# A graph layer and a mixture of experts on one core: the result is built up in the output tensor itself

## What is computed

```
x = x + gnn(layernorm(x), edges, relations)
x = x + ffn(layernorm(x))

# ffn, for the rows xf [6250, 256] of one batch
_, idx = jax.lax.top_k(xf @ Wg + bg, 2)
mask = one_hot(idx, 8).sum(axis=-2)
h = gelu(einsum('td,edh->teh', xf, W1) + b1[None], approximate=False)
y = einsum('teh,ehd->ted', h, W2) + b2[None]
out = einsum('ted,te->td', y, mask)
```

## Time and profile before

| what | value |
|---|---|
| median of 3 runs | 1563.23 us (1562.03 to 1563.25) |
| the profiled execution's own time | 1562.57 us |
| its span, first to last instruction | 1560.7 us |
| time around the span | 1.87 us |
| expert part: first addition issued to last addition issued | 1219.7 to 1534.5 us |
| busy share of the span: PE, DVE, ACT, POOL | 83%, 65%, 47%, 64% |

### The profile page before, as it was taken

One profiled execution on the slowest core, in us unless ns is written; L12 is line 12 of the kernel. 1 busy time (PEld: TensorE's weight loads), 2 busy tenths in 40 slices (PEclk: granted clock), 3 DMA queues, 4 the chain that ended last, 5 costly groups with the idle time before them and its releaser, 6 DMA issues. The chain is left out here.

```text
span 1560.7 us, 36074 instructions
## 1 busy us (share of the span) xinstructions
PE 1292.3 (83%) x12887; PEld 1056.9 (68%) x12887; DVE 1013.0 (65%) x2768; ACT 732.4 (47%) x1489; POOL 993.0 (64%) x868
## 2 busy tenths in 40 slices
PE   1269998999999999998899998775572999999991
PEld 1145566777777777777777777665562899999990
DVE  7857765576677777777878886864344555555550
ACT  6424453555455555554334342322131767676660
POOL 2077764676667777777777777777732455555551
PEclk9659998999999999999999999887675999999996
DMA  9686632444444555454544543443933466555556
GB/s 292 177 208 188 182 89 84 140 135 127 132 121 134 141 138 148 132 146 119 142 129 133 140 134 109 116 125 115 328 82 96 70 96 96 94 95 91 96 79 185
DMA packets 132379, 209.99 MB, mean 135 GB/s; under 512 B 26552, under 2 KB 99837, under 8 KB 130919
## 3 DMA queue, kind: packets, MB, share of 16 engines
q0 software_dynamic: 60032, 112.63, 30.7%
q1 hardware_dynamic: 72167, 94.97, 20.9%
HBM read 158.70 MB, written 57.76 MB: 139 GB/s over the span
## 5 line engine op out<-in xcount | busy, mean ns | idle before, releaser
L716 POOL DMA_INDIRECT ring<-h_table,idx x648 | 680.4, 1050 | 296.0 <-issue 211.3
L1728 PE MATMUL P<-hs,amat 128*126 128x512 f16 (+4 forms) x1568 | 403.6, 391 | 0.0
L833 ACT ACTIVATE amat<-P 128x300 f16<-128x300 f32 (+4 forms) x440 | 175.9, 445 | 253.7 <-PE P L1715 252.2
L770 POOL DMA_INDIRECT out_rows<-yo,xrows x112 | 177.0, 1580 | 162.2 <-DVE yo L1592 110.0
L1728 PEld LDWEIGHTS P<-hs,amat 128*126 128x126 f16 (+4 forms) x1568 | 182.4, 130 | 92.9 <-issue 7.8
L1710 PE MATMUL P<-cone,lone 128*128 128x294 f16 (+4 forms) x920 | 182.0, 294 | 44.7 <-ACT amat L833 39.0
L725 POOL DMA_INDIRECT expert_rows<-xrow,slots x100 | 126.3, 1263 | 67.9 <-DVE slots L1335 38.1
L1583 DVE SCALAR_TENSOR_TENSOR gl<-gT,scales,gh 128x512 f16<-128x512 f32 x112 | 84.2, 752 | 127.7 <-ACT gh L960 127.7
L1192 DVE TENSOR_TENSOR cone<-src_t,twice 128x1176 f16<-128x1176 f16 (+4 forms) x230 | 164.4, 715 | 0.0
L1942 PE MATMUL P<-xh,w_all 128*128 128x256 f16 x896 | 157.8, 275 | 0.0
L1955 PE MATMUL P<-w_all,gh 128*128 x896 | 149.8, 273 | 0.7 <-DVE gl L1583 0.7
(11 more groups left out here) (244 smaller groups left out, 2751.4 us busy)
## 6 DMA issues: line engine op xcount, KB each, us to landing
raw<-in_L_ffn_W_dram SPq DMA_DIRECT2D x32, 512.0 KB
xrows<-expert_rows SPq DMA_DIRECT2D x56, 257.0 KB, 3.1
ring<-h_table,idx POOLq DMA_INDIRECT x648
w_parts<-parts SPq DMA_DIRECT2D x16, 512.0 KB
w_all<-w_parts SPq DMA_DIRECT2D x8, 1024.0 KB, 20.2
h_in<-h_table SPq DMA_DIRECT2D x25, 250.0 KB
x<-in_x_dram SPq DMA_DIRECT2D x25, 250.0 KB
out_rows<-x SPq DMA_DIRECT2D x25, 250.0 KB
```

The source lines that it names most:

```text
L716: nc.gpsimd.indirect_dma_start(out=ring[:, r, j, :], out_offset=None, in_=h_dram, in_offset=bass.IndirectOffsetOnAxis(ap=idx[:, slot, g * ...
L770: nc.gpsimd.indirect_dma_start(out=out_dram, out_offset=bass.IndirectOffsetOnAxis(ap=xrows[:, b % XR, j, D:D + 1].bitcast(I32), axis=0), i ...
L833: nc.scalar.activation(amat[:, b % 2, :, s * aw:(s + 1) * aw], bank[:, 0:HIS * aw].rearrange("p (h w) -> p h w", w=aw), ACT.Copy).then_inc ...
L1728: nc.tensor.matmul(both, amat[:, b % 2, hi, 0:used], hs[:, hi, :], start=(hi == 0), stop=False)
```

## The change

The kernel's own output takes the place of `out_rows` everywhere: SP stores the residual rows to `out`, and POOL adds the experts' rows to `out`. As `out` has no rows beyond 6250, each of the 112 indirect transfers gets a bound of 6249 (`bounds_check=N - 1`), held in a register, with `oob_is_err=False`: a row whose number lies above the bound is left out. The transfer that zeroed the extra rows, the extra rows themselves, and the copy at the end with its wait are gone. SP's last act is now the wait for the last additions, which stood ahead of the copy before. No other instruction of any engine changes or changes its place: the same waits stand between the same instructions.

```diff
-PADS = TB
...
-    out_dram = nc.dram_tensor("out_rows", [N + PADS, D], F32).ap()
...
-            sp.dma_start(out_dram[N:N + PADS, :].rearrange("(j p) d -> p j d", p=128), pads[:, :, 0:D]).then_inc(s_init, 16)
...
-                sp.dma_start(node_rows(out_dram, i), x1[:, :, :]).then_inc(x_stored, 16)
+                sp.dma_start(node_rows(out, i), x1[:, :, :]).then_inc(x_stored, 16)
...
-            sp.wait_ge(s_init, 16 * (NE + 2))
+            sp.wait_ge(s_init, 16 * (NE + 1))
...
             for n in range(2):
                 sp.wait_ge(y_added[n], 32 * ((BLOCKS + 1 - n) // 2))
-            flat_out = out.rearrange("n d -> (n d)").rearrange("(a m) -> a m", m=1000)
-            flat_rows = out_dram[0:N, :].rearrange("n d -> (n d)").rearrange("(a m) -> a m", m=1000)
-            sp.dma_start(flat_out, flat_rows).then_inc(out_written, 16)
-            sp.wait_ge(out_written, 16)
...
                 for j in range(2):
                     nc.gpsimd.indirect_dma_start(
-                        out=out_dram, out_offset=bass.IndirectOffsetOnAxis(ap=xrows[:, b % XR, j, D:D + 1].bitcast(I32), axis=0),
-                        in_=yo[:, b % 2, j, :], in_offset=None, compute_op=ALU.add).then_inc(y_added[b % 2], 16)
+                        out=out, out_offset=bass.IndirectOffsetOnAxis(ap=xrows[:, b % XR, j, D:D + 1].bitcast(I32), axis=0),
+                        in_=yo[:, b % 2, j, :], in_offset=None, compute_op=ALU.add,
+                        bounds_check=N - 1, oob_is_err=False).then_inc(y_added[b % 2], 16)
```

More of the change, by code:

```diff
@@ L500, in gnn_ffn_kernel @@
             tx_done xh_ready xl_ready w1_ready l1_done gelu_done g_high g_low l2_done y_out firsts_ready
-            out_written dve_chain late_chain
+            dve_chain late_chain
         """.split()
@@ L514, in gnn_ffn_kernel @@
          tx_done, xh_ready, xl_ready, w1_ready, l1_done, gelu_done, g_high, g_low, l2_done, y_out, firsts_ready,
-         out_written, dve_chain, late_chain) = [sem(n) for n in names]
+         dve_chain, late_chain) = [sem(n) for n in names]
         s_nat = [sem(f"s_nat{n}") for n in range(3)]
```

## The result

The changed kernel takes 1542.54 us in the median of 6 runs (1534.12 to 1553.89), the kernel before 1562.22 (1558.48 to 1563.25, 6 runs). The ratio is 0.9879, with a 95% interval of 0.985 to 0.9907: 19 us less, between 15 and 23. The prediction was 1540.5 us, within 1534.0 to 1544.5, so the time lies 2 us above it and inside the range. Over all runs of this study both kernels scatter by 15 us and more, so the steps are read from the profiles.

What follows compares the result with a forecast made beforehand. The prediction took PE to set the pace in the expert part and the copy alone to fill the end; -22.3 + 0.9 - 1.0 - 0.3 = -22.7 us from 1563.23 gave 1540.5 us, range 1534.0 to 1544.5.

Steps and rivals of the forecast that it cites:

- (a): End of the kernel: with the copy gone, SP's wait for the additions becomes the last thing, -22.3 us.
- (b): Bound test on POOL's additions: 0.15 us each, covered in steady blocks, +0.9 us for six in the tail (0 to +3.2).
- (c): Pad rows left out: two tail landings shorten by half the packet time, 2 x 0.5 = -1.0 us.
- the 16 to 18 of the forecast: Tail: expected us for the chain from block 53's second addition to the end, 16.75 before the change.
- the first rival: Tail: skipped additions are nearly free, chain 12 to 13 us, time 1531 to 1538; chance 0.20.
- My test by the number of packets: Software queue, expert part: 14,292 packets if left-out rows have none; 16,128 would mean skipping saves nothing on the DMA engines.
- The rival of nearly free skips: Tail: skipped additions lose most of their landings, perhaps part of POOL's time; 1531 to 1538 us, chance 0.20.
- (d): Ahead of the expert part: without zeroing the spare rows, first gathers may come forward, -0.3 us (0 to -1.1).
- My condition that a move of over 2 us would mean an overlooked cause: Expert part's start: first addition expected at 1218.6 to 1219.7; moving over 2 us means something upstream isn't unchanged.
- a dear bound: POOL's additions: the test costs more but within POOL's slack, 0.7 us at most; 1543 to 1560 us, chance 0.08.
- POOL as the bound and a slower kernel: Expert part: test above 0.70 us an addition makes POOL set the pace, gain gone at 0.9 us; chance 0.04.

## Why the prediction held, and where it didn't

**(a) The copy, -22.3 us.** The length of the copy was right, and the step that failed is "Nothing lies beside it, so here the share of the copy on the path is all of it", with "SP's wait for the additions [...] becomes the last thing". POOL's DRAIN had ended 4.6 us after the additions landed, under the copy; now it is the end, 5.8 us behind SP in the changed kernel. The term's net is 22.3 - 5.8 = 16.5 us. The experiments without the copy and with another last instruction on POOL show it. The rows for it could have been had: the instructions of the program's end, with their start and duration, are in the trace of the kernel before, but they count as no engine's busy time, and I read only what was busy. Additions to the output tensor land no later than those to the scratch tensor: from block 53's second addition to block 54's first are 4.73 us, and 4.83 in the kernel before with the same bound.

**(b) The bound, +0.9 us in the tail.** The comparison's price is nothing: an addition takes 1.56 us with and without. The more software work for each row that the prediction drew from the Trainium skill ("DMA: Bandwidth & Descriptors", section "SWDGE vs HWDGE vs iDMA") shows in no run; the section states a pair of descriptors for a DMA operation, and that each row is one was the prediction's reading, which the 128 + 16 packets of an addition fit. What the bound does cost is 0.5 us between DVE's result and a block's first addition, since its register's setting took over the wait. POOL's slack covers that in the steady blocks, as I had said of any such price; in the tail it counts once, for block 53, which waits for DVE. So +0.5.

**(c) Skipped rows, -1.0 us.** Measured 1.0 for each of the two landings, so -2.0 up to SP's release: about the whole of the packets' time, where I had taken half. The chain from block 53's second addition to that release is 14.8 us, below the 16 to 18 of the forecast and above the 12 to 13 of the first rival. But the end follows POOL's last addition and not its landing, so block 55's microsecond is one that SP waits longer for the DRAIN, and only block 54's shortens the time. My test by the number of packets was built on a wrong idea: the number stayed at 16,128 and the packets became short. The rival of nearly free skips is answered with it: POOL spends the full time on skipped rows, and the landing keeps 1.2 to 1.3 us behind POOL's 1.56. The Trainium skill ("DMA: Bandwidth & Descriptors", section "Anatomy of one DMA") puts most of a transfer's fixed 2 us down to the receipt of the write. No such share fell away: the landing became 1.0 us shorter, and the 1.1 us by which the packets' time fell account for that. What the 1.2 to 1.3 us that are left consist of, no run shows.

**(d) The zeroing, -0.3 us.** Not settled: the start of the expert part moved by 3.4 us between the two profiles, by up to 1.7 us between profiles of one kernel, and by 5.1 and 8.5 us within the kernels with and without the zeroing. My condition that a move of over 2 us would mean an overlooked cause was too strict for a single profile.

With the terms as measured, -16.5 + 0.5 - 2.0 = -18.0 us. Counted by what ends last it is the same: the copy's removal -17.5 (22.3, less the 4.6 and the 0.2 us that POOL's DRAIN and the end behind it take back), the displaced wait +0.5, one landing -1.0. The profiles differ by 18.0 us from DVE's first result on. This lies in the measured -15 to -23 and within a microsecond of the median ratio's -19. The forecast of -22.7 was 4 to 5 us too much. That the time fell within the range is luck: it did because the range reached 4 us upwards for quite another reason, a dear bound, and because the median of before over six runs lies 1.0 us below the one that the sum started from. From that start the terms as measured give 1563.23 - 18.0 = 1545.2 us, just outside the range. POOL as the bound and a slower kernel are refuted: POOL idles 2.25 us a block as before.

## What to carry to other kernels

When the last thing on the path is taken away, look at everything that it covered, and at each engine's last instructions too, which no busy time shows: the gain is the distance to the next thing that ends, not the length of what is removed. A wait stands on the instruction that comes first behind it; a register set inside a loop can draw the wait to itself and expose the handing over that the wait had hidden, so constants are set once ahead of the loop. Work without effect isn't free for being skipped: find out at run time that it isn't needed, or at least take it out of the chain.

## What the runs showed of the hardware

- POOL's DRAIN at the program's end runs until about 6.9 us after POOL's last instruction (6.7 in one kernel), after an addition as after a small write. The DRAIN of DVE took 0.76 us and that of ACT 0.75 in the changed kernel.
- In an indirect addition of 128 rows with a bound, a row above it takes POOL as long as a valid one and sends a packet of some bytes: 144 packets for an addition with and without valid rows. The packets of an addition took 1.20 us of the 16 engines in the tail of the kernel before, where every row is added, and 0.07 us with every row skipped.
- The bound's comparison has no price on POOL that these runs can see: 1.56 us in both kernels.
